# Windowed attention: the output product moved into free columns of a scores bank, behind the scores; the input row made ahead of the output row

## The reference

```
x = x + conv_ref(ln(x))          # conv_ref is the attention:
q, k, v = split(x_ln @ w_qkv + bias), windows of 8x8, shifted by 4, 8 heads of 16
q = l2norm(q) * exp(scale); k = l2norm(k)
attn = softmax(q @ k^T + position bias + shift mask)
out = (attn @ v) merged over heads @ w_proj + b_proj
```

## Time and profile before

| | us |
|---|---|
| median of 3 runs | 11034.17 |
| lowest and highest run | 11019.4, 11040.31 |
| the profiled execution's time | 11027.03 |
| its span, first to last instruction | 11025.2 |
| the attention stage (about 1080 to 3383 us of the span) | 2303 |
| DVE busy in the stage | 2036.01 |
| PE busy in the stage | 1797.78 |
| ACT busy in the stage | 1668.44 |

### The profile page before, as it was taken

How to read it: one execution, slowest core, us unless ns; L and a number is a source line. 1 busy time by engine, 2 the same in 40 slices (tenths; PEclk the granted TensorE clock), 3 DMA queues, 4 the chain that set the end, 5 groups by cost and what they waited for, 6 DMA issues and landing times. The chain is left out here.

```text
span 11025.2 us, 125122 instructions
## 1 busy us (share of the span) xinstructions
PE 4769.1 (43%) x29069; PEld 2965.3 (27%) x29069; DVE 5592.9 (51%) x14901; ACT 3867.4 (35%) x9265; POOL 6152.7 (56%) x6259
## 2 busy tenths in 40 slices
PE   0111777777775998784232232232222323323000
PEld 0111666666663554552011011011111101101000
DVE  9997988888886776552121121211211212112477
ACT  0011777777772555332121121121111212212255
POOL 0000444444441221676777777777777777777675
PEclk9755999998996999887666666666666666666555
DMA  0000111111112222553222222222222222222366
GB/s 21 0 0 36 36 32 35 35 32 35 32 35 78 62 61 59 142 147 74 44 47 49 40 51 45 41 51 43 45 48 45 47 44 45 50 40 48 137 237 240
DMA packets 1325844, 659.79 MB, mean 60 GB/s; under 512 B 1058255, under 2 KB 1239100, under 8 KB 1320764
## 3 DMA queue, kind: packets, MB, share of 16 engines
q1 hardware_dynamic: 1142396, 576.49, 19.2%
q0 software_dynamic: 183104, 80.22, 6.2%
HBM read 344.86 MB, written 313.71 MB: 60 GB/s over the span
## 5 line engine op out<-in xcount | busy, mean ns | idle before, releaser
L1843 POOL DMA_INDIRECT gr_rec<-rec,gr_idx x4096 | 3963.3, 968 | 1248.8 <-issue 1247.9
L1864 PE MATMUL gr_p_h<-gr_tT,gr_w 128*128 128x512 f32 x1568 | 848.0, 695 | 3682.3 <-ACT gr_hT L1898 3648.9
L1983 DVE TENSOR_SCALAR gr_pen<-gr_same 128x64 f32<-128x64 f32 x64 | 13.7, 215 | 3170.5 <-DMA gr_rec<-rec,gr_idx 3170.5
L1864 PEld LDWEIGHTS gr_p_h<-gr_tT,gr_w 128*128 128x128 f32 x1568 | 347.0, 226 | 4164.8 <-ACT gr_hT L1898 3734.0
L549 POOL TENSOR_TENSOR at_sq<-at_qk 128x256 f32<-128x256 f32 x392 | 263.9, 673 | 2121.3 <-ACT at_qk L591 2118.9
L1911 ACT ACTIVATE gr_ee<-gr_dd 128x512 f32<-128x512 f32 x64 | 40.3, 629 | 3598.4 <-DVE gr_dd L2002 3598.4
L1869 PE MATMUL gr_p_y<-gr_hT,gr_w 128*128 128x512 f32 x1568 | 688.9, 592 | 0.0
L1963 DVE STREAM_TRANSPOSE gr_z<-gr_yb 128x2048 f32<-128x2048 f32 x98 | 226.5, 2311 | 895.4 <-ACT gr_yb L1903 863.9
L1898 ACT ACTIVATE gr_hT<-gr_p_h,gr_b 128x512 f32<-128x512 f32 x784 | 517.8, 688 | 190.2 <-PE gr_p_h L1864 186.9
L2151 POOL DMA_INDIRECT cb_a<-scan,cb_idx x392 | 503.9, 1286 | 133.7 <-issue 121.1
L1347 POOL DMA_INDIRECT adst<-co_rec,co_idx x448 | 422.8, 944 | 202.5 <-issue 148.5
(11 more groups left out here) (364 smaller groups left out, 13262.2 us busy)
## 6 DMA issues: line engine op xcount, KB each, us to landing
y<-gr_z SPq DMA_DIRECT2D x392, 256.0 KB, 5.2
cb_y<-y SPq DMA_DIRECT2D x28, 3584.0 KB
gr_rec<-rec,gr_idx POOLq DMA_INDIRECT x4096, 2.4
scan<-gr_out SPq DMA_DIRECT2D x64, 768.0 KB, 3.5
at_xs<-in_x_win SPq DMA_DIRECT2D x56, 448.0 KB, 3.9
x<-at_x SPq DMA_DIRECT2D x56, 448.0 KB, 4.5
ff_x<-x SPq DMA_DIRECT2D x56, 448.0 KB, 3.3
x<-ff_x SPq DMA_DIRECT2D x784, 32.0 KB
```

The lines of the kernel that those rows point to most:

```text
L1843: nc.gpsimd.indirect_dma_start(out=rec[s][:, j, :], out_offset=None, in_=rec_dram, in_offset=bass.IndirectOffsetOnAxis(ap=idx[s][:, j:j + ...
L1864: nc.tensor.matmul(p_h[m % 4][:, :], w1[:, P * m:P * (m + 1)], tT[b.k][:, :], start=True, stop=True).then_inc(S["hp"], 1)
```

## The change

Four edits, all in the attention. `p_O` moves from the bank `p_tr` into columns 128 to 263 of the first scores bank. On PE the output product of t-1 is written behind the scores of t+1 rather than ahead of them. The waits follow: the output product no longer waits for `xT` and `oT` but for the logits of t; the scores now wait for `on` of t-2 too; the two transposes no longer wait for `on` of t-1. On DVE `xh` of t+4 is made ahead of `rc` and `on` of t-1. No operation is added or removed and no shape changes.

```diff
+        p_O = p_s[:, 0, P:P + GRP * VW].rearrange("p (g v) -> p g v", g=GRP)
-        p_O = p_tr[:, 320:320 + GRP * VW].rearrange("p (g v) -> p g v", g=GRP)
...
-                    if p.has(-1):
-                        p.wait("pT", -1)
-                        p.wait("v", -1)
-                        p.wait("xT", 3)
-                        p.wait("oT", -3)
-                        p.wait("on", -2, 2)
-                        for w in range(2):
-                            for g in range(GRP):
-                                mm = nc.tensor.matmul(p_O[64 * w:64 * w + 64, g, :], pT[r][:, g, 64 * w:64 * w + 64],
-                                                      vb[:, w, g, :], start=True, stop=True)
-                        mm.then_inc(S["outp"], 1)
                     if p.has(1):
                         p.wait("kn", 1)
                         p.wait("logit", 0, 3, 1)
+                        p.wait("on", -2, 2)
                         p.wait("x1", -4)
...
+                    if p.has(-1):
+                        p.wait("pT", -1)
+                        p.wait("v", -1)
+                        p.wait("logit", 0, 3, 1)
+                        p.wait("on", -2, 2)
+                        for w in range(2):
+                            for g in range(GRP):
+                                mm = nc.tensor.matmul(p_O[64 * w:64 * w + 64, g, :], pT[r][:, g, 64 * w:64 * w + 64],
+                                                      vb[:, w, g, :], start=True, stop=True)
+                        mm.then_inc(S["outp"], 1)
...
                     if p.has(-2):
                         p.wait("on", -2, 2)
-                        p.wait("on", -1, 2)
                         p.wait("xT", 3)
...
                         p.wait("xh", 4)
-                        p.wait("on", -1, 2)
                         p.wait("xT", 3)
...
+                    if p.has(4):
+                        strip, s, j = p.strip(4)
...
+                        nc.vector.tensor_scalar(xh[p.slot(4)][:, :], xs[s][:, j, :], mv[s][:, j, 0:1], rstd[s][:, j:j + 1],
+                                                ALU.subtract, ALU.mult).then_inc(S["xh"], 1)
                     if p.has(-1):
...
-                        nc.vector.tensor_scalar(xh[p.slot(4)][:, :], xs[s][:, j, :], mv[s][:, j, 0:1], rstd[s][:, j:j + 1],
-                                                ALU.subtract, ALU.mult).then_inc(S["xh"], 1)
```

More of the change, by code:

```diff
@@ L488, in emit @@
                         mm.then_inc(S["qkvp"], 1)
-                    if p.has(-1):
-                        r = p.slot(-1)
-                        vb = vbd[(p.u - 1) % PPS]
-                        p.wait("pT", -1)
-                        p.wait("v", -1)
-                        p.wait("xT", 3)
-                        p.wait("oT", -3)
-                        p.wait("on", -2, 2)
-                        for w in range(2):
-                            for g in range(GRP):
-                                mm = nc.tensor.matmul(p_O[64 * w:64 * w + 64, g, :], pT[r][:, g, 64 * w:64 * w + 64],
-                                                      vb[:, w, g, :], start=True, stop=True)
-                        mm.then_inc(S["outp"], 1)
                     if p.has(1):
@@ L514, in emit @@
                         mm.then_inc(S["scores"], 1)
+                    if p.has(-1):
+                        r = p.slot(-1)
+                        vb = vbd[(p.u - 1) % PPS]
+                        p.wait("pT", -1)
[7 more added lines that the diff above has]
+                        mm.then_inc(S["outp"], 1)
                     if p.has(-3):
@@ L712, in emit @@
                         nc.vector.tensor_tensor(lm[q][:, :, :], lg[q][:, :, :], top, ALU.subtract).then_inc(S["logit"], 1)
+                    if p.has(4):
+                        strip, s, j = p.strip(4)
+                        if j == 0 or p.u == -4:
+                            v.wait_ge(S["xrstd"], 2 * (strip + 1))
+                        p.wait("xTp", 2)
+                        nc.vector.tensor_scalar(xh[p.slot(4)][:, :], xs[s][:, j, :], mv[s][:, j, 0:1], rstd[s][:, j:j + 1],
+                                                ALU.subtract, ALU.mult).then_inc(S["xh"], 1)
                     if p.has(-1):
```

## The result

The changed kernel takes 11106.12 us in the median of 5 runs (11081.09 to 11115.43), the kernel before 11034.17: ratio 1.0063, 95% interval 1.0046 to 1.008, some 70 us slower. The forecast was 11021, faster by 0.12%, with a range up to 11066.

A forecast was written before the change was run, and what follows sets the result against it. DVE was taken to bound the attention stage (busy 2036 of 2303 us). Terms -8 (late trips), -10 (waits for `rs`) and +5 (new waits at `rc`) gave -13 us: 11034 to 11021 us, range 10992 to 11066.

The forecast's parts named there:

- At most about 51 us can be won: DVE's waits for other engines: 32.2 us at `rc` for the output product, 18.9 us at `qkn` for `rs`.
- Every engine's busy time stays: Whole attention stage: no operation is added or dropped, so only the times at which DVE's inputs are ready move.
- The waits for `rs`: DVE ahead of `qkn`: `rs` comes up to 0.21 us earlier, 10 us won of 18.9, bounds 0 and 15.5.
- The late trips: DVE at `rc` where PE is late: 33 waits shortened by 0.25 us each, 8 us won, bounds 2 to 13.
- The trip that was worked through: PE late, low clock from 2099.41, `rc` waiting 1.32 us; gain put at 0.05 to 0.38 us, 0.25 taken.
- New waits at `rc`: DVE waits 0.6 us where the low clock hits scores and output product; 5 us lost, bounds 4 and 67.
- the lower bound: Added waiting at `rc`: 7 slow scores blocks times 0.6 us, 4 us; 5 was taken, near this end.
- rival B: Output product too late: one 2.5 us PE idle stretch ahead of the scores, `rc` waits; 11076 us at 100 trips; 0.22.
- DVE's busy time stays: Profile check on the attention stage: DVE busy stays 2036 us; a change over 10 us makes the base wrong.
- PE's waits at the scores: Profile check on PE: with the wait of `oT` for `on` gone, waits gather there, around 300 us or more.
- signs towards B: Profile checks: `rc` waits more than 60 times; output products of 1.2 us and more are common.
- 0.24 us of margin at `rc`: DVE-led trip at full clock: output product ends at 2097.95, `rc` asks at 2098.19 behind `xh`, so no wait.

## Why the prediction was wrong

**The bound.** Right: DVE bounds the stage, and PE's 275.1 us of waiting for `on` were worth almost nothing. "At most about 51 us can be won" was never put to the test by this change; what the sum had no term for was a loss on DVE itself.

**"Every engine's busy time stays."** This step failed first. The prediction costed the move of `xh` at nothing: it looked at what `xh` needs, not at what had stood in its cover. `qkn` has four waits (the order rows of DVE ahead of the prediction list them), and `xh` had hidden them. The term that the sum lacked is 389 steps of 0.066 us, 26 us; by the ratios with and without the three waits it is some 41 us, with 17 to 64 possible. The 26 us are in no wait view: the step is between instructions that overlap, so the loss is counted in DVE's busy time. They are the largest part of the 43 us by which that grew; the rest was not traced to one place.

**The waits for `rs`, -10 us.** Right in size, 18.9 to 5.8 us, and given back at once by the 13 us more of "issue" ahead of the same instruction: nothing in all.

**The late trips, -8 us.** Too much. The trip that was worked through was taken at the clock of before. With the low clock from the scores on, as in the rows at 1616.51, PE is late by the whole trip, and the waits behind a fast product, 18 of the 60, average 1.6 us instead of 1.32 less 0.25. They are fewer but longer: 29.6 us in all, where the 33 waits of before took 32.2, so some 3 us won and not 8.

**New waits at `rc`, +5 us.** This is the second step that failed, and by its size. The mechanism was named and priced about right: 0.6 us each; measured 42 waits of `rc` behind a product of over 1.05 us, 22 us in all, 0.5 each (49 and 30 us over the whole stage). What failed is the choice of the lower bound, "since the low clock sets in after the waiting". 55 of 392 output products were slow, 34 before. That was rival B, at 22%: its place and its price were right, and its count of 70 to 100 trips too high; it came below the loss measured because the hand-over at `qkn` was in no rival.

**The clock.** In these rows the low clock follows PE's idle stretch: two of 1.44 and 0.99 us, then low at the norm sums; one of 3.21 us, then low at the scores. That is not so behind every stretch. In the changed kernel 17 of the 36 output products whose scores came behind 3 us of idling or more were slow, 35 of 198 behind 1 to 3 us, and 1 of 156 behind less. Holding PE busy there took most of the waits away, but only once the three waits at `qkn` were gone. The rule of the Trainium skill that the prediction cited ("TensorE: Matmul & The Clock Gate", section "HAM oscillation — how this bites in real kernels") says that bursts behind waits start cold. The rows shown agree: the output product took 1.52 us behind 3.21 us of idling and 0.92 with fillers; the counts say that many bursts behind a stretch did not.

**What the profile was to show.** "DVE's busy time stays" was the check named for a wrong base, with 10 us as its mark; it moved by 43. PE's waits at the scores were put at 300 us or more and measured 518.9. Both signs towards B came, the first of them just: `rc` waited 60 times in the window and 69 times in the whole stage, where more than 60 was the mark, and 47 output products took 1.2 us or more, 14 before. The 0.24 us of margin at `rc` were right: with `xh` put back it was gone, and 293 trips waited.

## What to carry to other kernels

An instruction that moves takes its cover with it: list for each neighbour the semaphore waits that had hidden behind it, and drop those that another wait implies before reordering. When waits on an engine off the bound are merged into one, ask what stands first behind the merged stretch and who waits for it, since that is what runs at the low clock. A few products of filler in such a stretch can be worth more than the reordering, as long as the loop's body stays small; here 5 of them per strip paid in three of the four kernels that they were tried in, and not in the changed kernel with its four waits.

## What the runs showed of the hardware

- Three semaphore waits more on a DVE instruction (`qkn`) that follows right on `on`, whose operands come from `rc`, cost 0.06 us a time (0.27 against 0.21 us), and behind the 0.34 us instruction `xh` nothing (0.25 in both). Without them DVE's wait for itself at a strip's end fell from 0.33 to 0.15 us too (17.3 us in 53 waits, 7.4 in 49); why, the runs don't show.
- With 30 and 34 products more in the loop's body, PE stood still 3.4 to 3.7 us at each turn; with 10 to 14 it did not. DVE waits 3.0 to 3.2 us at each turn in the versions where PE doesn't, and 3.4 to 3.7 where it does. Where the limit lies, and what it is, stays open.
- Where PE's clock was low decided which instruction was slow. In the version with the product in the probabilities' bank, 5 products more per strip raised the granted clock from 0.89 to 0.92 and made the kernel 0.36% faster; in the changed kernel with its four waits the same 5 left it at 0.89.
